# Loading and ordering of the first two layers: packed input transfers, a split mixing step, and a changed order on four engines

## The chip, the core and the metric

The kernel runs on one core of a Trainium2 chip. The metric is the device time of one execution in microseconds (us); the lower the better. The core has five engines with instruction streams of their own, which meet only at semaphores: TensorE (PE, matmuls, with its weight loads, PEld, shown apart), VectorE (DVE), ScalarE (ACT), GpSimd (POOL) and SyncE (SP), which here only issues DMA transfers. All data starts in HBM and ends there.

## The reference

Eight sequences of 128 tokens with 128 features go through four residual layers. `cond_8` (8 x 8) steers all of them:

```python
# layer 0: a base product plus a mixture of eight rank-16 adapters
out = einsum('btc,oc->bto', x, W_base) + b_base
lora = einsum('bter,eor,be->bto', einsum('btc,erc->bter', x, As), Bs, w)
x = x + out + lora * 2
# layer 1: eight weight matrices, masked, mixed per sequence
w_bot = einsum('bg,got->bot', y, weight * mask)
x = x + einsum('bnt,bot->bno', x, w_bot) + bias
# layer 2: gated MLP (128 -> 512 -> 128), top 2 of 8 experts per sequence, plus a shared one
x = x + sum_top2(w_e * mlp_e(x)) + mlp_shared(x)
# layer 3: gated MLP (128 -> 256 -> 128) of the single best expert, with biases
x = x + mlp3_best(x)
```

## The kernel before

Everything is held transposed: features on the 128 partitions, the 1024 tokens (8 sequences of 128) along the row, in two halves of 512. Each engine's program is written out by hand, in order, and each `wait_ge` names a semaphore; nothing is reordered by a scheduler.

**Layer 0.** The adapters and the base product are folded into one 128 x 128 matrix per sequence. VectorE (L363, sequences 0 to 3, in two instructions) and ScalarE (L272, sequences 4 to 7) scale the adapters' second factor into `b_mix`; TensorE's `mix0` (L575, three matmuls) multiplies by the first factor; VectorE's `weights0` (L374, once for each half) adds the base matrix plus identity, `base_i`, which GpSimd makes (L247). `product0` (L595, four matmuls for each half) applies the matrices to the tokens `x_t`, and ScalarE's `stream1` (L283) adds the bias.

**Layer 1.** `mix1_part` (L587) multiplies eight 128 x 128 blocks of the weights, four to a half, by a small spread-out matrix `mix1` of the conditions; VectorE's `weights1` (L382, once for each half) multiplies by the mask. `product1` (L603) needs both halves of these weights and its half of `x1_t`; VectorE's `stream2` (L424) makes the new tokens twice, rounded to the matmul's faster type (`x2_h`) and in full (`x2_t`); `stream2_rest` (L429) makes the difference `x2_l`.

**The shared expert of layer 2** runs first among the experts. Its three weight blocks (gate, up, down; n = 0, 1, 2) are split in the same way: ScalarE's `round_shared(n)` (L278) makes the high part, GpSimd's `shared_low_part(n)` (L250) the low part. TensorE's first matmul pair (L635 and L636, `shared_high(0, 0)`) needs `x2_h` and both parts of block 0; the next pair, `shared_high(0, 1)`, needs both parts of block 1 (`sh_high` and `sh_low` at 2). Then the products with `x2_l` follow (L644), and the down products (L651 to L654).

**Routing** runs on VectorE: `route_first` and `leave_first` (L392 to L397), then `route_second` (L401 to L404, whose last instruction signals `val2_ready`) and `rank_second` (L408). GpSimd waits for `val2_ready`, does `shared_low_part(0)`, then turns the ranks into expert numbers (L256, `routed`), then does blocks 1 and 2. SyncE waits for `routed` before it loads the experts' weights (L193, L201). ScalarE's exponential (L286) needs `route_second` too.

**The rest**, from about 27 us on, is one pass over the sequences with the routed experts (L664, L674) and layer 3 (L687, L701), with weights loaded two sequences ahead. The change does not touch it.

**Loads.** SyncE's queue issues, in order: `head` (the adapters and the conditions; its first 64 partitions, the others come from ScalarE's queue), `rest` (conditions for the routing, base matrix, mask, biases), the first half of layer 1's weights with `mix1` (L180), the first half of the tokens (L181), the second half of the weights (L182), the second half of the tokens (L183), and the shared expert's down block (L184). ScalarE's queue issues its half of `head`, and after its `b_mix` work the gate block and the up block (L274). Ahead of all its work TensorE runs six warm-up matmuls on a tile of zeros (L570) that VectorE sets (L357).

Of the kernel before, what the change touches and what calls it, by code (L numbers as in the profile page):

```python
# [5 lines left out]
B, S, C = 8, 128, 128  # L6
E = 8
R = 16
# [21 lines left out]
W1A = MIX // 2 + B * OH  # L30


def build(nc, x, head, rest_in, w1, shared, skill, layer3, out):
# [8 lines left out]
    with ctx:  # L42
# [33 lines left out]
        a_sb, b_sb, wcol = head_sb[:, 0:C], head_sb[:, C:2 * C], head_sb[:, 2 * C:HEAD]  # L76
        rest_sb = sb("rest_sb", [128, REST])
        condb, base_t, mask_t, b0col, b1col, bias3 = (rest_sb[:, at:at + n] for at, n in REST_PARTS)
# [3 lines left out]
        w1_sb = sb("w1_sb", [128, MIX + B * OH])  # L82
        mix1 = w1_sb[:, MIX // 2:W1A]
# [40 lines left out]
        x_loaded = [sem("x_loaded0"), sem("x_loaded1")]  # L124
        w1_in = [sem("w1_in0"), sem("w1_in1")]
        shared_in = [sem(f"shared_in{n}") for n in range(3)]
# [11 lines left out]
        warm_ready = sem("warm_ready")  # L138
# [98 lines left out]
        def _(pool):  # L237
# [20 lines left out]
            shared_low_part(1)  # L258
            shared_low_part(2)
# [7 lines left out]
        def _(act):  # L267
            act.dma_start(head_sb[64:128, :], head[64:128, :]).then_inc(head_in, 16)
            act.preload_act_table(ACT.Exp)
            act.wait_ge(head_in, 32)  # L270
            for b in range(HALF, B):
                act.activation(b_mix[:, b, :], b_sb, ACT.Copy, scale=wcol[:, b:b + 1]).then_inc(b_mixed2, 1)  # L272
            for n in range(2):
                act.dma_start(shared_sb[:, n, :], shared[:, n, :]).then_inc(shared_in[n], 16)  # L274

            def round_shared(n):
                act.wait_ge(shared_in[n], 16)
                act.activation(shared_h[:, n, :], shared_sb[:, n, :], ACT.Copy).then_inc(sh_high, 1)  # L278
# [63 lines left out]
        def _(dve):  # L342
# [14 lines left out]
            dve.memset(warm[:, :], 0.0).then_inc(warm_ready, 1)  # L357
            cond3 = condb.rearrange("p (b e) -> p b e", e=E)

            dve.wait_ge(head_in, 32)  # L360
# [5 lines left out]
            dve.wait_ge(rest_landed, 16)  # L366
# [11 lines left out]
            def weights1(h):  # L378

                dve.wait_ge(p1_done, h + 1)  # L380
# [186 lines left out]
        def _(pe):  # L567
            pe.wait_ge(warm_ready, 1)
            for _ in range(WARM):
                pe.matmul(bank[6][:, 0:128], warm[:, :], warm[:, :], start=True, stop=True)  # L570
# [9 lines left out]
            def mix1_part(h):  # L580

                pe.wait_ge(w1_in[0], 16)
                if h == 1:
                    pe.wait_ge(w1_in[1], 16)
                for n in range(OL // 2):
                    at = h * W1A + C * n
                    mm = pe.matmul(bank[5 + h][:, 128 * n:128 * (n + 1)], w1_sb[:, at:at + C], mix1, start=True, stop=True)  # L587
                mm.then_inc(p1_done, 1)
# [215 lines left out]
```

## Time and profile before

| | |
|---|---|
| time, median of 3 runs (lowest, highest) | 88.49 us (88.18, 88.63) |
| the profiled execution's own time | 87.75 us |
| its span, first to last instruction | 85.9 us |
| TensorE busy | 82.2 us (96%) of 618 matmul passes |
| VectorE, ScalarE, GpSimd busy | 47.7, 30.8, 15.5 us |
| read from HBM, written to it | 17.95 MB, 0.52 MB |

The profiled execution lies 0.74 us below the median of the runs. A matmul on fp32 data appears as two passes in the trace, so the six warm-up matmuls are twelve entries; one on the rounded type is one entry. A line of the time view stands for a row of like instructions: its second number is the time from the first one's start to the last one's end, and "xN" their count. Matmul entries overlap each other, so the start of a weight load is the better mark of TensorE's place in its program.

### The profile page before, as it was taken

The numbers are of one execution on the slowest core, as the hardware profiler recorded it, in microseconds if no ns is written. First come the engines' busy times: TensorE is split into PE (matmuls) and PEld (weight loads), VectorE is DVE, ScalarE is ACT, GpSimd is POOL, SyncE is SP. The second block draws the span as 40 slices with busy tenths as digits, with TensorE's granted clock in tenths as the row PEclk, the third lists the DMA queues.
The fourth block names the chain that finished last, engine by engine and source line by source line (L and its number), as shares of the span: only waits on it lengthen the run. The fifth ranks groups of instructions, "written<-read, shape, count | busy, mean of one in ns | idle before, by whom it ended". The sixth has DMA issues, their size and how long they took to land.

```text
span 85.9 us, 1921 instructions
## 1 busy us (share of the span) xinstructions
PE 82.2 (96%) x618; PEld 77.5 (90%) x618; DVE 47.7 (55%) x110; ACT 30.8 (36%) x55; POOL 15.5 (18%) x20
## 2 busy tenths in 40 slices
PE   5999899999999999999999999999999999999980
PEld 5978898888888999999999999999999999999970
DVE  0489439853533999329338447456465564563270
ACT  3702783777555520221221222212402402408320
POOL 3010773098666900000000000000000000000000
PEclk9999999999999999999999999999999999999999
DMA  0899318799920000596679899879998988717102
GB/s 7 214 358 312 143 23 326 266 325 425 402 72 0 0 0 4 132 331 272 206 269 328 253 296 306 302 264 312 337 346 316 299 279 315 289 41 163 50 0 61
DMA packets 5927, 18.57 MB, mean 216 GB/s; under 512 B 672, under 2 KB 1952, under 8 KB 5920
## 3 DMA queue, kind: packets, MB, share of 16 engines
q1 hardware_dynamic: 5552, 17.88, 61.0%
q10 hardware_dynamic: 368, 0.59, 2.1%
q8 instruction: 4, 0.07, 0.3%
q14 instruction: 3, 0.02, 0.2%
HBM read 17.95 MB, written 0.52 MB: 215 GB/s over the span
## 4 chain that ended last, share of the span: by engine, by line
PE 87%; DMA 6%; SPq 3%; issue 1%; DVE 0%
PE bank L664 33%; PE bank L674 17%; PE bank L687 9%; DMA w_sb<-in_w 6%; PE bank L701 4%; PE bank L635 4%; PE bank L636 4%; PE bank L644 4%; PE bank L603 2%; PE bank L652 2%; PE bank L654 2%; PE bank L651 2%; PE bank L587 1%; PE bank L595 1%; SPq L179 1%; SPq L178 1%
## 5 line engine op out<-in xcount | busy, mean ns | idle before, releaser
L664 PE MATMUL bank<-x_t,pair_w 128*128 128x128 f32 (+1 forms) x256 | 31.2, 275 | 0.0
L664 PEld LDWEIGHTS bank<-x_t,pair_w 128*128 128x128 f32 x256 | 30.0, 192 | 0.2
L300 ACT ACTIVATE gelu<-bank 128x512 f32<-128x512 f32 x24 | 14.2, 596 | 32.5 <-PE bank L664 27.8
L468 DVE SCALAR_TENSOR_TENSOR hid<-gelu,wsel,bank 128x512 f32<-128x512 f32 x16 | 12.0, 748 | 18.5 <-PE bank L664 18.4
L674 PE MATMUL bank<-hid,pair_w 128*128 128x128 f32 x128 | 16.9, 275 | 0.0
L674 PEld LDWEIGHTS bank<-hid,pair_w 128*128 128x128 f32 x128 | 15.7, 192 | 0.1
L263 POOL TENSOR_TENSOR hid_l<-hid,hid_h 128x512 fp32r<-128x512 f32 x8 | 10.2, 1289 | 6.3 <-ACT hid_h L323 6.3
L466 DVE TENSOR_TENSOR hid<-gelu,bank 128x512 f32<-128x512 f32 x8 | 5.5, 688 | 6.3 <-ACT gelu L300 3.8
L687 PE MATMUL bank<-x_t,w 128*128 128x128 f32 x64 | 8.7, 276 | 0.0
L687 PEld LDWEIGHTS bank<-x_t,w 128*128 128x128 f32 x64 | 7.9, 192 | 0.2 <-issue 0.2
L635 PE MATMUL bank<-x_h,shared_h 128*128 128x512 f32 x16 | 6.3, 396 | 0.0
L636 PE MATMUL bank<-x_h,shared_l 128*128 128x512 f32 x16 | 6.2, 390 | 0.0
L304 ACT ACTIVATE tanh<-half 128x256 f32<-128x256 f32 x6 | 2.5, 416 | 10.1 <-DVE half L497 10.1
L323 ACT ACTIVATE hid_h<-hid 128x512 fp32r<-128x512 f32 x8 | 5.0, 627 | 1.0 <-DVE hid L466 0.9
L701 PE MATMUL bank<-hid,w 128*128 128x128 f32 x32 | 4.9, 279 | 0.0
L644 PE MATMUL bank<-x_l,shared_h 128*128 128x512 f32 x16 | 4.8, 389 | 0.0
L250 POOL TENSOR_TENSOR shared_l<-shared_sb,shared_h 128x512 fp32r<-128x512 f32 x3 | 3.8, 1279 | 4.9 <-ACT shared_h L278 4.8
L701 PEld LDWEIGHTS bank<-hid,w 128*128 128x128 f32 x32 | 4.2, 191 | 0.1
L504 DVE SCALAR_TENSOR_TENSOR gate<-bank,bsel,half 128x128 f32<-128x128 f32 x12 | 3.7, 347 | 0.6
L570 PE MATMUL bank<-warm 128*128 128x128 f32 x12 | 2.9, 434 | 1.0 <-DVE warm L357 1.0
L497 DVE TENSOR_SCALAR half<-bank,bsel 128x128 f32<-128x128 f32 x12 | 3.6, 343 | 0.0
L570 PEld LDWEIGHTS bank<-warm 128*128 128x128 f32 x12 | 2.6, 329 | 1.0 <-DVE warm L357 1.0
(67 smaller groups left out, 76.6 us busy)
## 6 DMA issues: line engine op xcount, KB each, us to landing
pair_w<-in_skill SPq DMA_DIRECT2D x16, 768.0 KB, 5.8
w<-in_layer SPq DMA_DIRECT2D x8, 384.0 KB, 6.0
x_t<-in_x SPq DMA_DIRECT2D x2, 256.0 KB, 5.0
shared_sb<-in_shared ACTq DMA_DIRECT2D x2, 256.0 KB, 5.5
out_x<-out_sb SPq DMA_DIRECT2D x8, 64.0 KB, 4.6
w_sb<-in_w SPq DMA_DIRECT2D x1, 320.0 KB, 3.7
w_sb<-in_w SPq DMA_DIRECT2D x1, 256.0 KB, 5.6
shared_sb<-in_shared SPq DMA_DIRECT2D x1, 256.0 KB, 6.4
```

What stands on the lines that cost most here:

```text
L263: pool.tensor_tensor(hid_l[:, k % 3, :], hid[:, k % 2, :], hid_h[:, k % 3, :].bitcast(fp32), ALU.subtract).then_inc(hid_low, 1)
L300: act.activation(gelu[:, n, :], ps[:, :], ACT.Gelu_apprx_tanh).then_inc(gelu_ready, 1)
L466: dve.tensor_tensor(hid[:, n, :], gelu[:, n, :], shu_ps(k)[:, :], ALU.mult).then_inc(hid_ready, 1)
L468: dve.scalar_tensor_tensor(hid[:, n, :], gelu[:, n, :], wsel[:, bass.DynSlice(weight, 1)], u_ps[n][:, :], ALU.mult, ALU.mult).then_inc(hid ...
L570: pe.matmul(bank[6][:, 0:128], warm[:, :], warm[:, :], start=True, stop=True)
L635: pe.matmul(ps[:, :], shared_h[:, m, 128 * t:128 * (t + 1)], high, start=True, stop=False)
L636: pe.matmul(ps[:, :], shared_l[:, m, 128 * t:128 * (t + 1)], high, start=False, stop=False)
L644: pe.matmul(ps[:, :], shared_h[:, m, 128 * t:128 * (t + 1)], x2_l[:, N * h:N * (h + 1)], start=False, stop=True).then_inc(done, 1)
L664: mm = pe.matmul(ps[:, S * t:S * (t + 1)], pair_w[:, slot, n, 128 * t:128 * (t + 1)], x2_t[:, columns(b)], start=True, stop=True)
L674: mm = pe.matmul(acc_ps[:, 0:S], pair_w[:, slot, 2, C * t:C * (t + 1)], hid[:, k, S * t:S * (t + 1)], start=(k == 0 and t == 0), stop=(k = ...
L687: pe.matmul(ps[:, S * c:S * (c + 1)], w3[:, q, n, 128 * c:128 * (c + 1)], x3_t[:, q, :], start=True, stop=True).then_inc(done, 1)
L701: mm = pe.matmul(out_ps[:, 0:S], w3[:, q, 2, C * c:C * (c + 1)], hid3[:, q, c, :], start=(c == 0), stop=(c == HC - 1))
```

## The change

- **Loads.** `head` is one transfer over 128 partitions, issued by SyncE, and now holds the conditions for the routing too. ScalarE's queue starts with a new array `first`: `mix1` and the first two of layer 1's eight weight blocks. `rest` loses the routing's conditions and gains the other six blocks. The tokens are one transfer, third on SyncE's queue. After its `b_mix` work ScalarE's queue issues gate and up as one transfer, then down. So there are six transfers where there were ten; the bytes are the same, 2.2 MB.
- **Warm-up.** The zeros are a broadcast of a constant that exists before the program starts; VectorE's instruction and the wait for it go.
- **TensorE.** Two mixing blocks come ahead of `mix0`, the other six behind it, and `product0(0)` and `product0(1)` follow without a mixing part between them. Both wait for all tokens.
- **VectorE.** `route_second` and `rank_second` move behind `weights0(1)`, `weights1(0)` and `weights1(1)`.
- **ScalarE.** `round_shared(0)` comes first, then `stream1(0)`, the exponential, `stream1(1)`, and only then `round_shared(1)`.
- **GpSimd.** `shared_low_part(2)` also waits for the first half of `x2_l`.

```diff
-HEAD = 2 * C + B
-_WIDTHS = [B * E, C, C, 1, 1, (2 * HC + 1) * E]
+HEAD = 2 * C + B + B * E
+_WIDTHS = [C, C, 1, 1, (2 * HC + 1) * E]
-MIX = OL * C
+EARLY = 2
+FIRST = B * OH + EARLY * C
...
-        warm = sb("warm", [128, 128])
+        zeros = nc.const_aps.tensor(0.0, [128, 128], fp32)
...
-            sp.dma_start(head_sb[0:64, :], head[0:64, :]).then_inc(head_in, 16)
+            sp.dma_start(head_sb[:, :], head[:, :]).then_inc(head_in, 16)
             sp.dma_start(rest_sb[:, :], rest_in[:, :]).then_inc(rest_landed, 16)
-            sp.dma_start(w1_sb[:, 0:W1A], w1[:, 0:W1A]).then_inc(w1_in[0], 16)
-            sp.dma_start(x_t[:, 0:N], x[:, 0:N]).then_inc(x_loaded[0], 16)
-            sp.dma_start(w1_sb[:, W1A:MIX + B * OH], w1[:, W1A:MIX + B * OH]).then_inc(w1_in[1], 16)
-            sp.dma_start(x_t[:, N:2 * N], x[:, N:2 * N]).then_inc(x_loaded[1], 16)
-            sp.dma_start(shared_sb[:, 2, :], shared[:, 2, :]).then_inc(shared_in[2], 16)
+            sp.dma_start(x_t[:, :], x[:, :]).then_inc(x_loaded, 16)
...
             shared_low_part(1)
+            pool.wait_ge(x2_low, 1)
             shared_low_part(2)
...
-            act.dma_start(head_sb[64:128, :], head[64:128, :]).then_inc(head_in, 16)
+            act.dma_start(first_sb[:, :], first[:, :]).then_inc(first_in, 16)
...
-            for n in range(2):
-                act.dma_start(shared_sb[:, n, :], shared[:, n, :]).then_inc(shared_in[n], 16)
+            act.dma_start(shared_sb[:, 0:2, :], shared[:, 0:2, :]).then_inc(gate_up_in, 16)
+            act.dma_start(shared_sb[:, 2, :], shared[:, 2, :]).then_inc(shared_down_in, 16)
...
-            act.wait_ge(shifted_ready, 2)
-            act.activation(expo_all[:, :], shifted_all[:, :], ACT.Exp).then_inc(expo_ready, 1)
             round_shared(0)
             act.wait_ge(rest_landed, 16)
             stream1(0)
+            act.wait_ge(shifted_ready, 2)
+            act.activation(expo_all[:, :], shifted_all[:, :], ACT.Exp).then_inc(expo_ready, 1)
+            stream1(1)
             round_shared(1)
-            stream1(1)
             round_shared(2)
...
             weights0(0)
-            route_second()
-            rank_second()
             weights0(1)
             weights1(0)
             weights1(1)
+            route_second()
+            rank_second()
...
-            pe.wait_ge(head_in, 32)
+            pe.wait_ge(first_in, 16)
+            mix1_part(0, EARLY)
+            pe.wait_ge(head_in, 16)
             mix0(0, HALF // 2, b_mixed, 1)
             mix0(HALF // 2, HALF, b_mixed, 2)
             mix0(HALF, B, b_mixed2, HALF)
-            mix1_part(0)
+            pe.wait_ge(rest_landed, 16)
+            mix1_part(EARLY, OL)
             product0(0)
-            mix1_part(1)
             product0(1)
```

TensorE's rows from the first mixing work to the first product of layer 1. Before (L575 is `mix0`, L587 the mixing of layer 1, L595 `product0`):

```order
L575 MATMUL bank<-b_mix,head_sb 128x256 [waits b_mixed,head_in]
L575 MATMUL bank<-b_mix,head_sb 128x256 [waits b_mixed]
L575 MATMUL bank<-b_mix,head_sb 128x512 [waits b_mixed2]
L587 MATMUL bank<-w_sb 128x128 [waits w1_in0]
L587 MATMUL bank<-w_sb 128x128 x3
L595 MATMUL bank<-x_t,p 128x128 [waits x_loaded0,p0_ready]
L595 MATMUL bank<-x_t,p 128x128 x3
L587 MATMUL bank<-w_sb 128x128 [waits w1_in1,w1_in0]
L587 MATMUL bank<-w_sb 128x128 x3
L595 MATMUL bank<-x_t,p 128x128 [waits x_loaded1,p0_ready]
```

And of the changed kernel (L570 is `mix0`, L581 the mixing of layer 1, L590 `product0`):

```order
L581 MATMUL bank<-first_sb 128x128 [waits first_in]
L581 MATMUL bank<-first_sb 128x128
L570 MATMUL bank<-b_mix,head_sb 128x256 [waits b_mixed,head_in]
L570 MATMUL bank<-b_mix,head_sb 128x256 [waits b_mixed]
L570 MATMUL bank<-b_mix,head_sb 128x512 [waits b_mixed2]
L581 MATMUL bank<-first_sb,rest_sb 128x128 [waits rest_landed]
L581 MATMUL bank<-first_sb,rest_sb 128x128 x5
L590 MATMUL bank<-x_t,p 128x128 [waits x_loaded,p0_ready]
L590 MATMUL bank<-x_t,p 128x128 x3
L590 MATMUL bank<-x_t,p 128x128 [waits x_loaded,p0_ready]
```

Two blocks moved ahead of `mix0`, the four of the second half moved ahead of `product0(0)`, and one wait for all tokens stands where two waits for half of them stood.

ScalarE's rows between its `b_mix` work and the table load, before (L286 is the exponential, L278 `round_shared`, L283 `stream1`):

```order
L286 ACTIVATE expo_all<-shifted_all 128x72 [waits shifted_ready]
L278 ACTIVATE shared_h<-shared_sb 128x512 [waits shared_in0]
L283 ACTIVATE x_t<-bank,rest_sb 128x512 [waits x1_done,rest_landed]
L278 ACTIVATE shared_h<-shared_sb 128x512 [waits shared_in1]
L283 ACTIVATE x_t<-bank,rest_sb 128x512 [waits x1_done]
L278 ACTIVATE shared_h<-shared_sb 128x512 [waits shared_in2]
```

And of the changed kernel (L274 is `round_shared`, L279 `stream1`, L285 the exponential):

```order
L274 ACTIVATE shared_h<-shared_sb 128x512 [waits gate_up_in]
L279 ACTIVATE x_t<-bank,rest_sb 128x512 [waits x1_done,rest_landed]
L285 ACTIVATE expo_all<-shifted_all 128x72 [waits shifted_ready]
L279 ACTIVATE x_t<-bank,rest_sb 128x512 [waits x1_done]
L274 ACTIVATE shared_h<-shared_sb 128x512 [waits gate_up_in]
L274 ACTIVATE shared_h<-shared_sb 128x512 [waits shared_down_in]
```

The second `round_shared` now stands behind the second `stream1`, and the exponential between the two `stream1`.

## Rows read from the trace of the kernel before

**Rows 1.** Chain that ended last, in order: start us, us, what.
```profile
3.17 5.58 DMA w_sb<-in_w
8.74 0.14 issue
8.88 1.13 PE bank L587 x8
```

**Rows 2.** Stretches: us, busy time and count by engine, PEclk, DMA share, GB/s.
```profile
2.00:4.00 2.00, 2.00 (x11) 1.94 (x10) 0.76 (x2) 1.40 (x4) 0.00 (x0) 1.00 0.80 194
4.00:6.50 2.50, 2.50 (x6) 1.75 (x7) 2.10 (x7) 0.47 (x2) 0.46 (x1) 1.00 0.93 349
6.50:8.00 1.50, 1.50 (x13) 1.32 (x12) 1.40 (x7) 0.26 (x1) 0.00 (x0) 1.00 0.86 276
8.00:10.00 2.00, 1.74 (x15) 1.46 (x13) 0.77 (x2) 1.60 (x3) 0.96 (x1) 1.00 0.71 274
12.90:25.00 12.10, 12.10 (x56) 10.01 (x56) 7.29 (x11) 7.53 (x14) 7.22 (x6) 1.00 0.86 322
```

**Rows 3.** Groups to 14 us, by form: xcount | busy us, mean ns.
```profile
L570 PE MATMUL bank<-warm 128*128 128x128 f32 x12 | 2.9, 434 | 1.0 <-DVE warm L357 1.0
...
L595 PE MATMUL bank<-x_t,p 128*128 128x128 f32 x16 | 2.2, 280 | 0.0
```

**Rows 4.** TensorE's weight loads in time: start us, us, engine, line.
```profile
3.73 2.20 PEld L575 LDWEIGHTS bank<-b_mix,head_sb 128*128 128x128 f32 x6
...
6.25 0.19 PEld L587 LDWEIGHTS bank<-w_sb 128*128 128x128 f32 x1 [0.31 <-DMA w_sb<-in_w]
...
7.46 0.97 PEld L595 LDWEIGHTS bank<-x_t,p 128*128 128x128 f32 x8
...
8.85 0.97 PEld L587 LDWEIGHTS bank<-w_sb 128*128 128x128 f32 x8 [0.42 <-issue]
...
9.94 0.97 PEld L595 LDWEIGHTS bank<-x_t,p 128*128 128x128 f32 x8
...
10.83 2.08 PEld L603 LDWEIGHTS bank<-x_t,p 128*128 128x128 f32 x16
...
13.18 0.19 PEld L635 LDWEIGHTS bank<-x_h,shared_h 128*128 128x128 f32 x1
```

**Rows 5.** The other engines in the same stretch, in time.
```profile
4.22 0.46 POOL L247 TENSOR_TENSOR base_i<-rest_sb,ident 128x128 f32<-128x128 f32 x1 [2.67 <-DMA rest_sb<-in_rest]
...
6.51 0.21 DVE L401 TENSOR_REDUCE m<-rest 128x8 f32<-128x64 f32 x1
...
7.35 0.22 DVE L408 TENSOR_REDUCE rank<-val 128x8 f32<-128x64 f32 x1
...
9.04 1.28 POOL L250 TENSOR_TENSOR shared_l<-shared_sb,shared_h 128x512 fp32r<-128x512 f32 x1 [4.36 <-ACT shared_h L278]
...
10.05 0.69 DVE L382 TENSOR_TENSOR p<-bank,rest_sb 128x512 f32<-128x512 f32 x1 [1.28 <-PE bank L587]
...
10.69 1.27 POOL L250 TENSOR_TENSOR shared_l<-shared_sb,shared_h 128x512 fp32r<-128x512 f32 x1
...
11.14 0.69 ACT L283 ACTIVATE x_t<-bank,rest_sb 128x512 f32<-128x512 f32 x1 [0.90 <-PE bank L595]
11.72 0.62 ACT L278 ACTIVATE shared_h<-shared_sb 128x512 fp32r<-128x512 f32 x1
...
12.42 1.29 POOL L250 TENSOR_TENSOR shared_l<-shared_sb,shared_h 128x512 fp32r<-128x512 f32 x1 [0.46 <-ACT shared_h L278]
```

**Rows 6.** Transfers: queue, KB each, us from issue to landing (median).
```profile
x_t<-in_x SPq DMA_DIRECT2D x2, 256.0 KB, 5.0
shared_sb<-in_shared ACTq DMA_DIRECT2D x2, 256.0 KB, 5.5
...
head_sb<-in_head ACTq DMA_DIRECT2D x1, 66.0 KB, 2.4
```

**Rows 7.** SyncE's first load of an expert, in time.
```profile
11.58 1.48 SPq L193 DMA_DIRECT2D pair_w<-in_skill  x2
```

More of the change, by code:

```diff
@@ L21, with build @@
 LOWEST = -3.0e38
-HEAD = 2 * C + B
-_WIDTHS = [B * E, C, C, 1, 1, (2 * HC + 1) * E]
+HEAD = 2 * C + B + B * E
+_WIDTHS = [C, C, 1, 1, (2 * HC + 1) * E]
 REST_PARTS = [(sum(_WIDTHS[:n]), width) for n, width in enumerate(_WIDTHS)]
 REST = sum(_WIDTHS)
-MIX = OL * C
+EARLY = 2
+FIRST = B * OH + EARLY * C
 WARM = 6
-W1A = MIX // 2 + B * OH
-def build(nc, x, head, rest_in, w1, shared, skill, layer3, out):
+def build(nc, x, first, head, rest_in, shared, skill, layer3, out):
     fp32, fp32r, i32 = mybir.dt.float32, mybir.dt.float32r, mybir.dt.int32
@@ L75, in build @@
         head_sb = sb("head_sb", [128, HEAD])
-        a_sb, b_sb, wcol = head_sb[:, 0:C], head_sb[:, C:2 * C], head_sb[:, 2 * C:HEAD]
-        rest_sb = sb("rest_sb", [128, REST])
-        condb, base_t, mask_t, b0col, b1col, bias3 = (rest_sb[:, at:at + n] for at, n in REST_PARTS)
+        a_sb, b_sb, wcol = head_sb[:, 0:C], head_sb[:, C:2 * C], head_sb[:, 2 * C:2 * C + B]
+        condb = head_sb[:, 2 * C + B:HEAD]
+        first_sb = sb("first_sb", [128, FIRST])
+        mix1 = first_sb[:, 0:B * OH]
+        rest_sb = sb("rest_sb", [128, REST + (OL - EARLY) * C])
+        base_t, mask_t, b0col, b1col, bias3 = (rest_sb[:, at:at + n] for at, n in REST_PARTS)
         bias_t = bias3.rearrange("p (n e) -> p n e", e=E)
         base_i = sb("base_i", [128, C])
-        warm = sb("warm", [128, 128])
-        w1_sb = sb("w1_sb", [128, MIX + B * OH])
-        mix1 = w1_sb[:, MIX // 2:W1A]
+        zeros = nc.const_aps.tensor(0.0, [128, 128], fp32)
         p1 = sb("p1", [C, B, C])
@@ L123, in build @@
         head_in, rest_landed = sem("head_in"), sem("rest_landed")
-        x_loaded = [sem("x_loaded0"), sem("x_loaded1")]
-        w1_in = [sem("w1_in0"), sem("w1_in1")]
-        shared_in = [sem(f"shared_in{n}") for n in range(3)]
+        first_in, x_loaded = sem("first_in"), sem("x_loaded")
+        gate_up_in, shared_down_in = sem("gate_up_in"), sem("shared_down_in")
         sh_high, sh_low = sem("sh_high"), sem("sh_low")
@@ L355, in over_b @@
                 return a.unsqueeze(1).broadcast_to([128, B, a.shape[1]])
-            dve.memset(warm[:, :], 0.0).then_inc(warm_ready, 1)
             cond3 = condb.rearrange("p (b e) -> p b e", e=E)
-            dve.wait_ge(head_in, 32)
+            dve.wait_ge(head_in, 16)
             for first in range(0, HALF, HALF // 2):
@@ L378, in weights1 @@
             def weights1(h):
+                dve.wait_ge(rest_landed, 16)
                 dve.wait_ge(p1_done, h + 1)
@@ L567, in _ @@
         def _(pe):
-            pe.wait_ge(warm_ready, 1)
             for _ in range(WARM):
-                pe.matmul(bank[6][:, 0:128], warm[:, :], warm[:, :], start=True, stop=True)
+                pe.matmul(bank[6][:, 0:128], zeros, zeros, start=True, stop=True)
             def mix0(first, last, mixed, count):
@@ L578, in mix0, with mix1_part @@
                     mm.then_inc(p0_done, 1)
[L580 to L588, printed above, removed]
+            def mix1_part(begin, end):
+                for a in range(begin, end):
+                    h, n = a // (OL // 2), a % (OL // 2)
+                    weights = (first_sb[:, B * OH + C * a:B * OH + C * (a + 1)] if a < EARLY else
+                               rest_sb[:, REST + C * (a - EARLY):REST + C * (a - EARLY + 1)])
+                    mm = pe.matmul(bank[5 + h][:, 128 * n:128 * (n + 1)], weights, mix1, start=True, stop=True)
+                    if n == OL // 2 - 1:
+                        mm.then_inc(p1_done, 1)
             def product0(h):
                 pe.wait_ge(p0_ready, h + 1)
-                pe.wait_ge(x_loaded[h], 16)
+                pe.wait_ge(x_loaded, 16)
                 for n in range(HALF):
```

16 lines of the change are left out of this document (7 added, 9 removed).

## The prediction

> **What bounds the kernel now.** I read the chain of waits first, then the busy time in stretches, then the order in time of each engine up to 14 us. From 12.9 to 25 us TensorE is busy for all of 12.1 us [rows 2], and the chain holds nothing but TensorE from there to the last matmul. So whatever moves the start of the shared expert's stream moves the end by the same amount, and nothing behind it gives it back. The kernel has a front, up to the weight load of `shared_high(0, 1)` at 13.18 us [rows 4], and a tail that is carried along. The change edits only the front. I use that one weight load as the finish line, because its operands are the ones that the change makes later.
>
> In the front the chain is a transfer, the second half of layer 1's weights, issued at 3.17 us and there 5.58 us later, and then TensorE [rows 1]. From the weight load of `mix1_part(1)` at 8.85 the marks are 9.94, 10.83 and 13.18 [rows 4]. Ahead of it TensorE was nearly full as well: `mix0` from 3.73, the first mixing part at 6.25, `product0(0)` at 7.46, whose eight passes end near 8.4. That is the first thing to see: before 8.85 TensorE waits only some 0.4 us, the gap in front of that row. A better load order can win 0.4 us and little more.
>
> The second thing is the clock. The granted clock reads 1.00 in every stretch [rows 2], but the durations say otherwise: a 128-column fp32 pass takes 434 ns in the warm-up and 280 ns in `product0` [rows 3], and twelve warm-up passes fill 2.9 us, 244 ns each, where eight passes of `product0` load their weights in 0.97 us [rows 4], 112 ns from one to the next. So I take TensorE to be at 1.2 GHz, the lower of its two levels, through the warm-up and most of `mix0`, and at 2.4 GHz from about 6 us, where a weight load has come down to 0.19 us. A pass placed ahead of 6 us costs twice what it costs behind it.
>
> **The change part by part.**
>
> *First landings.* `head` was two transfers of 66 KB (68,000 bytes each), the later one there 2.4 us after its issue at 0.7, so at 3.1 [rows 6]. Now `head` is 168,000 bytes and `first`, 197,000, moves beside it, all on the same engines. The extra 230,000 bytes need 0.6 to 1.2 us at 349 to 194 GB/s [rows 2], of which `head` bears about half. I take 3.8 for both (3.4 to 4.3).
>
> *TensorE up to the products.* The warm-up no longer waits for VectorE and starts 0.2 us earlier, which only lengthens the wait for the first data. At 3.8 the two mixing blocks run: four passes at 244 ns [rows 3], 1.0 us. `mix0` thus starts at about 4.8, 1.0 us later than in rows 4; `b_mix` is ready by then. Of the 1.0 us of slow work pushed past the clock's rise half is given back, so `mix0` ends about 0.5 us later, at 7.1, where 6.6 was its end before. Then six blocks, twelve passes at 112 ns, 1.35 us: TensorE reaches `product0(0)` at 8.5. Moving the two blocks forward used an idle slot that was not there; what it bought is 0.45 us of fast work behind, and what it cost is 1.0 us of slow work in front, half of it recovered, so about nothing.
>
> *The tokens.* They are third on SyncE's queue and both products wait for all of them. Ahead of or with them go `head`, `first` and `rest` (546,000 bytes) and the tokens themselves (524,000): 1,435,000 bytes, and up to 524,000 of gate and up, which ScalarE's queue adds from about 5.2. The kernel before had moved 388,000 by 4.0, 1,260,000 by 6.5, 1,674,000 by 8.0 and 2,222,000 by 10 (each the GB/s by the length of the stretch [rows 2]). On that curve 1,435,000 are reached at 7.1 and 1,959,000 at 9.0; with 0.5 us until the semaphore, the tokens land between 7.6 and 9.5. The stretch up to 4.0 should be better than 194 GB/s, since two large transfers are queued from the start: at 349 GB/s it is 1.0 us of head start. Against this stands that a transfer is there only when the slowest engine has finished. I take 8.4, the upper middle, and keep 7.2 and 9.4.
>
> *A rule of the Trainium skill.* The rows show 194 GB/s while the small transfers ran and 349 GB/s just after [rows 2], which speaks for fewer and longer ones. The Trainium skill ("DMA: Bandwidth & Descriptors", Rules for kernel authors) says the same, that many small transfers should be coalesced and that two over disjoint halves of the partitions are pointless; by its fixed cost of about 2 us and 436 GB/s, an estimate for 1.43 MB is 5.3 us from the first issue, so tokens at 6.0. The same page of the Trainium skill also says (Issuing engines are not separate DMA queues) that the queues of all engines interleave on the same 16 DMA engines, and that is what speaks against the change: gate and up take their share while the tokens are under way. No row shows the tokens alone.
>
> *Start of the products.* TensorE is ready at 8.5, the tokens are there at 8.4: call it S = 8.5. `product0(1)` follows 0.9 us later without a pause, at P = 9.4, where it was 9.94. From there the old spacing to the finish line is 3.24 us (9.94 to 13.18 [rows 4]), which gives 12.64: a gain of 0.54.
>
> *Rounding of the up block.* The finish line also needs both parts of block 1. ScalarE now does `stream1(1)` first. It came 1.2 us after the weight load of `product0(1)` (9.94 to 11.14), the next rounding 0.58 us later, GpSimd's part 0.70 us after that, and took 1.28 us [rows 5]. From P that is 9.4 + 1.2 + 0.58 + 0.70 + 1.28 = 13.16. Before, the part was done at 11.96, 1.2 us ahead of its use; that cover is gone.
>
> *GpSimd's own queue.* It may be later still. `route_second` now stands behind `weights1(1)`. That instruction came 1.2 us after the first weight load of its four blocks (8.85 to 10.05) and took 0.69 [rows 5]; its blocks now load from 7.6, so it runs from 8.8 to 9.5. `route_second` takes 0.84 (6.51 to 7.35): `val2_ready` at 10.34. There GpSimd starts block 0, and block 1 follows 1.65 us later (9.04 to 10.69), with the ranks between: 11.99, done at 13.27, and TensorE sees it at about 13.32. The same order delays the ScalarE exponential (needs `shifted_ready` at about 9.8, while `stream1(1)` could start at 10.6: hidden) and `routed`, from 10.6 to about 11.85. SyncE's first load of an expert moves from 11.58 [rows 7] to about 12.9; its consumer sits behind 25 us and its load took under 6, so this is free.
>
> *The rest.* `base_i` waits for a larger `rest`, there at 4.1 before [rows 5], about 5.4 now; `weights0(0)` needs it at 6.3. GpSimd's block 2 waits for `x2_l`, near 14 us, and has until the first down product, behind 18 us. Gate and up land near 9.0; `round_shared(0)` takes 0.6 and `stream1(0)` is wanted at 9.7. All at nothing, each with cover of 0.1 to 4 us; the thinnest is gate and up, which cost from 9.2 on.
>
> **The sum.** 13.32 against 13.18: 0.54 won on TensorE, 0.68 lost in the wait for the up block's low part, +0.14 us. On the profiled execution that is a span of 86.04 and a time of 87.9; the median of the runs lies 0.74 above the profiled one, so I forecast 88.49 + 0.15 = 88.65.
>
> **The rivals.**
>
> *Tokens late (slower).* If the tokens land after 8.5, every microsecond counts in full, and TensorE starts from a standstill, 1.09 instead of 0.9 to the next row [rows 4]. At 9.3 the products start at 9.35, P is 10.44 and the finish line 10.44 + 3.76 + 0.05 = 14.25: +1.1, 89.6. For it: the transfer that ended the front before took 5.6 us [rows 1], the half-token transfers 5.0 [rows 6], and now more bytes stand ahead. Against: the slack 194 GB/s at the beginning. It decides from 8.5.
>
> *Both early (faster).* With tokens at 7.5 and a clock that rises right behind the warm-up, `mix0` ends at about 6.1 (ScalarE's last `b_mix` is what it waits for), six blocks end at 7.5, S = 7.6, P = 8.6, and the finish line is 12.4: -0.75, 87.75. For it are the stretches at 349 GB/s; it needs the early rise too, and the rows put that at 6. The coalescing rule of the Trainium skill ("DMA: Bandwidth & Descriptors", Rules for kernel authors) points this way, but for the tokens alone.
>
> *Low part in time (faster).* If `shared_high(0, 1)` does not wait, the gain of 0.54 stays: 87.95. For it is only that GpSimd's spans are rough; against it is that the rounding stands behind `stream1(1)` in the program.
>
> *Clock late (slower).* Slow work now lies in front. If the rise comes at 7.5, `mix0` is done at 7.9 and the products start at 9.25, +0.85: 89.35. The rows show one rise only. The Trainium skill ("TensorE: Matmul & The Clock Gate", Part 1) states that the throttled clock is the default and that activity releases it; by that rule the earlier warm-up does no harm, and no run here shows when the rise comes in another execution.
>
> **How the numbers follow.** My forecast, 88.3 to 88.9: 0.46. Tokens late: 0.22. Clock late: 0.08. Both early: 0.15. Low part in time: 0.09. The range that holds 8 in 10 runs from 87.9 to 89.4; left out are most of "both early" and the upper half of the two slow cases. A measurement of this kernel can tell about 0.5%, 0.44 us, from no change. So faster 0.24, same 0.46, slower 0.30.
>
> **What would show it.** In the changed kernel's trace: the tokens' landing and the weight load of the first `product0` at about 8.5; `product0(1)` 0.9 behind it; an idle TensorE of 0.5 to 0.7 us between the first and the second pair of L632 and L633, released by GpSimd's `shared_l`; that `shared_l` started by ScalarE's rounding or by GpSimd's own queue at about 12; no TensorE gap behind it. I am wrong if TensorE stands idle ahead of `product0`, if the 128-column passes of the mixing are slow beyond 7 us, or if the second pair follows the first at once.

## The result and the profile after

| | before | changed |
|---|---|---|
| median over all executions beside each other | 88.28 us (14) | 87.61 us (14) |
| ratio of the changed kernel to the one before | | 0.991, 95% interval 0.989 to 0.994 |
| profiled execution: time, span | 87.75, 85.9 us | 87.69, 85.9 us |

The change makes the kernel faster by 0.9%, 0.7 to 0.8 us, and the time lies below the forecast range. The ratio leaves out executions more than 1.5% above the fastest of their kernel: three of the changed kernel's fourteen, at 88.53, 89.60 and 292.65 us, the last of unknown cause. A second series of twelve executions, beside 22 others of the kernel before (median 88.36), gave a median of 87.87 and a ratio of 0.995 (0.990 to 0.999), half the gain of the first series; the two intervals overlap.

The two profiled executions have the same span, although the medians are 0.67 us apart. That is the puzzle of this case, and the trace of the changed kernel alone doesn't solve it. First the busy time in stretches of the changed kernel (columns as in rows 2):

```profile
2.00:4.00 2.00, 1.67 (x9) 1.37 (x8) 0.20 (x1) 0.64 (x2) 0.00 (x0) 1.00 0.86 315
4.00:6.50 2.50, 2.50 (x10) 2.11 (x11) 2.06 (x9) 1.08 (x4) 0.46 (x1) 1.00 1.03 420
6.50:8.00 1.50, 1.50 (x12) 1.26 (x11) 1.39 (x3) 0.18 (x1) 0.00 (x0) 1.00 0.88 347
8.00:10.00 2.00, 2.00 (x20) 2.00 (x19) 1.78 (x7) 1.03 (x2) 0.00 (x0) 1.00 0.00 0
```

Where rows 2 have 194, 349, 276 and 274 GB/s, it is now 315, 420, 347 and nothing: the same 2.2 MB are over two microseconds earlier. The tokens land 4.8 us after their issue at 1.65, at 6.5 us.

The chain that ended last, changed kernel (start us, us, what; the finish line of the prediction is the wait that ends at 13.1):

```profile
0.72 3.23 DMA first_sb<-in_first
...
3.99 1.23 PE bank L581 x4
5.22 1.87 PE bank L570 x6
7.09 1.35 PE bank L581 x12
...
8.53 0.69 DVE p L377
...
9.72 0.24 DVE val L399
...
10.03 1.27 POOL shared_l L245
...
11.38 0.21 POOL chosen L251
...
11.67 1.30 POOL shared_l L245
...
13.10 0.47 PE bank L632
```

The landing of `first` at 3.95 us is the last one on it. Then it is TensorE's mixing work, VectorE's `weights1` and routing, and two of GpSimd's low parts: the chain that the prediction worked out, step for step. The weight loads of TensorE in time, where L581 is the mixing of layer 1, L570 `mix0`, L590 and L598 the products:

```profile
3.99 0.93 PEld L581 LDWEIGHTS bank<-first_sb 128*128 128x128 f32 x4 [0.63 <-DMA first_sb<-in_first]
...
4.80 1.46 PEld L570 LDWEIGHTS bank<-b_mix,head_sb 128*128 128x128 f32 x6
...
6.50 0.19 PEld L581 LDWEIGHTS bank<-first_sb,rest_sb 128*128 128x128 f32 x1 [0.24 <-issue]
...
8.15 1.87 PEld L590 LDWEIGHTS bank<-x_t,p 128*128 128x128 f32 x16
...
10.22 1.86 PEld L598 LDWEIGHTS bank<-x_t,p 128*128 128x128 f32 x16 [0.20 <-issue]
...
12.22 0.19 PEld L632 LDWEIGHTS bank<-x_h,shared_h 128*128 128x128 f32 x1
...
13.07 0.19 PEld L632 LDWEIGHTS bank<-x_h,shared_h 128*128 128x128 f32 x1 [0.55 <-issue]
```

The finish line is at 13.07 where rows 4 have it at 13.18. From 12.22 to 13.07 are 0.85 us where the kernel before needs 0.34: that is the forecast wait for block 1's low part.

### The profile page after: what moved, and what is told of

It is laid out like the page before. It is cut to its first block, busy times and chain, and to the rows that moved or that the text cites. A ratio compares the mean times of both kernels' runs of the same rounds, so it can differ in the third digit from the quotient of the medians.

```text
span 85.9 us, 1918 instructions
## 1 busy us (share of the span) xinstructions
PE 82.2 (96%) x618; PEld 77.3 (90%) x618; DVE 47.3 (55%) x109; ACT 30.7 (36%) x55; POOL 15.6 (18%) x20
## 4 chain that ended last, share of the span: by engine, by line
PE 87%; DMA 4%; POOL 3%; DVE 2%; issue 1%; DVEq 0%
PE bank L661 33%; PE bank L671 17%; PE bank L684 9%; PE bank L698 4%; PE bank L632 4%; PE bank L641 4%; PE bank L633 4%; DMA first_sb<-in_first 4%; PE bank L581 3%; POOL shared_l L245 3%; PE bank L570 2%; PE bank L649 2%; PE bank L648 2%; PE bank L651 2%; DVE p L377 1%
## 5 line engine op out<-in xcount | busy, mean ns | idle before, releaser
L632 PEld LDWEIGHTS bank<-x_h,shared_h 128*128 128x128 f32 x16 | 3.0, 188 | 1.2 <-issue 0.6
L564 PE MATMUL bank<-const-float32-0.0 128*128 128x128 f32 x12 | 2.9, 432 | 0.8 <-PEq L793 0.8
```

Source lines behind the costliest of these rows:

```text
L632: pe.matmul(ps[:, :], shared_h[:, m, 128 * t:128 * (t + 1)], high, start=True, stop=False)
```

## The experiments

All ratios are to runs of the kernel before on the same chip. I read the same few marks in every trace. The finish line is the weight load of `shared_high(0, 1)`; "mix0" is the time from the first to the last of its six weight loads, which is short where the clock rises early in it.

| kernel | mix0, us | first product0 | finish line | span | span less finish line |
|---|---|---|---|---|---|
| before, first trace | 2.20 | 7.46 | 13.18 | 85.9 | 72.7 |
| before_3rd | 1.40 | 8.47 | 13.72 | 86.5 | 72.8 |
| before_4th | 1.37 | 7.94 | 13.85 | 86.6 | 72.8 |
| changed, first trace | 1.46 | 8.15 | 13.07 | 85.9 | 72.8 |
| after_again | 2.25 | 9.96 | 14.88 | 87.5 | 72.6 |
| loads_only3 | 2.21 | 9.49 | 15.06 | 87.9 | 72.8 |
| loads_only_warm8 | 1.87 | 7.92 | 13.18 | 85.9 | 72.7 |
| mix0_first | 2.20 | 10.11 | 15.01 | 88.9 | 73.9 |
| mix0_first_warm8 | 1.52 | 8.23 | 13.14 | 85.8 | 72.7 |
| loads_early | 1.33 | 7.20 | 12.45 | 85.2 | 72.8 |
| loads_early_warm7 | 1.77 | 7.83 | 13.09 | 85.9 | 72.8 |
| both_early3 | 1.64 | 8.47 | 13.25 | 86.0 | 72.8 |
| split_loads | 2.25 | 10.04 | 14.96 | 87.6 | 72.6 |
| orders_only3 | 1.95 | 9.87 | 14.72 | 87.5 | 72.8 |

The last column is the first finding: in thirteen of fourteen traces the tail takes 72.6 to 72.8 us. (In mix0_first, whose profiled execution took 90.69 us, TensorE waits once more, 0.95 us at 56.3, for an expert's weights.) All differences lie in the front.

### The kernel before, twice more

> The kernel before once more, for a second profiled execution. Theory 1 (the profiled execution of before was an unusually good one: 87.75 us where 14 runs have a median of 88.28 and a lowest of 88.02): span 86.2 to 86.8, and the weight load of shared_high(0, 1) at 13.5 to 14.0 us instead of 13.18, because the second half of layer 1's weights lands later. Theory 2 (the front is the same in every execution, and the 0.7 us that the change won against the median came from elsewhere): finish line at 13.1 to 13.3 and the extra time behind it.

> A third profiled execution of the kernel before. Theory: its time follows the landing of the second half of layer 1's weights (8.7 us with span 85.9, 9.0 with span 86.5) and of the first half of the tokens (6.6 and 8.4); the rise of the clock, 6.0 and 4.2 us, doesn't show in it. A span of 86.2 to 86.8 with these landings at 8.8 to 9.3 and 6.6 to 8.6 supports it.

No edit. The times are 88.30 and 88.42 us, in the middle of the executions of before (median 88.4 and 88.36), where the first profiled one, at 87.75, was below the lowest of fourteen. In both the clock rises earlier than in the trace that I predicted from, and the finish line is later all the same, by 0.54 and 0.67 us. Weight loads of before_3rd, then of before_4th:

```profile
3.71 1.40 PEld L575 LDWEIGHTS bank<-b_mix,head_sb 128*128 128x128 f32 x6
...
8.47 0.97 PEld L595 LDWEIGHTS bank<-x_t,p 128*128 128x128 f32 x8 [1.65 <-DVE p L374]
...
10.49 0.97 PEld L595 LDWEIGHTS bank<-x_t,p 128*128 128x128 f32 x8 [0.16 <-issue]
...
13.72 0.19 PEld L635 LDWEIGHTS bank<-x_h,shared_h 128*128 128x128 f32 x1
```

```profile
6.42 0.97 PEld L587 LDWEIGHTS bank<-w_sb 128*128 128x128 f32 x8 [1.24 <-DMA w_sb<-in_w]
...
7.94 0.97 PEld L595 LDWEIGHTS bank<-x_t,p 128*128 128x128 f32 x8 [0.55 <-issue]
9.28 0.97 PEld L587 LDWEIGHTS bank<-w_sb 128*128 128x128 f32 x8 [0.37 <-issue]
```

The chain of before_3rd, and the transfers of layer 1's weights in before_4th (KB, us to landing):

```profile
2.69 5.68 DMA x_t<-in_x
...
8.51 1.13 PE bank L595 x8
9.63 0.89 PE bank L587 x8
```

```profile
w_sb<-in_w SPq DMA_DIRECT2D x1, 320.0 KB, 4.2
w_sb<-in_w SPq DMA_DIRECT2D x1, 256.0 KB, 6.0
```

TensorE idles 1.65 us ahead of `product0(0)` in the one (the first tokens land at 8.37; the label names VectorE's `weights0(0)`, which was done by 6.7), and 1.24, 0.55 and 0.37 us in the other. The late half of the weights needs 6.0 us where the first trace had 5.58 [rows 1]. So in both of these executions, which lie in the middle of the times, the kernel before waits for landings, and a clock that rises earlier only makes TensorE wait longer. The ranges of both expectations held. The reason given in the first one was only half right: in before_3rd it is the first half of the tokens that ends the wait, and the late half of the weights, there at 9.04, delays nothing. The long executions of the kernel before, 11 of 33 at 88.8 us or more in the two series beside mix0_first and after_again, were not traced, and what makes them long is not shown.

### The loads alone

> The changed kernel's six transfers with the orders of before on TensorE (mix0 first, a mixing part between the two products), VectorE, ScalarE and GpSimd; the constant-zero warm-up stays. If the gain of the change comes from the loads alone (tokens at 6.4 us in the changed kernel's trace, nothing is late), TensorE runs from mix0 at 4.2 us to the first layer without a pause and does not wait for the low part of block 1: finish line at 12.4 to 12.7, 87.0 to 87.2 us, 0.4 to 0.6 below the changed kernel. If the new orders carry the gain: at or above the changed kernel, 87.6 to 88.3.

```diff
-            pe.wait_ge(first_in, 16)
-            mix1_part(0, EARLY)
             pe.wait_ge(head_in, 16)
             mix0(0, HALF // 2, b_mixed, 1)
...
+            pe.wait_ge(first_in, 16)
...
-            mix1_part(EARLY, OL)
+            mix1_part(0, OL // 2)
             product0(0)
+            mix1_part(OL // 2, OL)
             product0(1)
```

This is against the changed kernel; on VectorE, ScalarE and GpSimd the lines that the change moved stand in their old places. Measured: 89.13 us in the median of 11, ten of them at 88.83 and above, one at 86.96. Neither reading had this. The finish line is at 15.06, and the cause is seen in TensorE's loads and in the chain:

```profile
4.42 2.21 PEld L569 LDWEIGHTS bank<-b_mix,head_sb 128*128 128x128 f32 x6 [1.05 <-DMA head_sb<-in_head]
```

```profile
4.45 3.75 PE bank L569 x6
8.20 1.71 PE bank L580 x8
9.90 1.07 PE bank L589 x8
```

Without the early blocks TensorE stands idle for 1.05 us between the warm-up and `mix0`, which needs `b_mix` and so begins 0.57 us behind the landing of `head` at 3.85. Then everything up to about 10 us runs at the pace of the 1.2 GHz level: `mix0` takes 3.75 us on the chain (1.87 in the changed kernel), eight passes of the mixing 1.71 (0.89 for eight in the row of loads_only_warm8 below). The granted clock reads 1.00 all the while.

> The changed kernel with the two early mixing blocks moved back behind mix0: TensorE waits for b_mix from the end of the warm-up at 3.6 us to about 4.4. Theory A (the gap keeps TensorE's clock at its lower level, as in the kernel with the loads alone, where mix0 began at 4.42 and passes stayed slow to about 10 us): first product0 at 9 us or later, finish line (weight load of shared_high(0, 1)) at 14.5 to 15.5, 89 us and more in most executions. Theory B (what cost that kernel its time was another of the old orders, not the gap): the blocks' place is worth nothing, 87.4 to 88.0 us, as the changed kernel.

> The same with eight warm-up matmuls instead of six, so that the warm-up ends at 4.6 us and touches mix0. Theory A (what counts is that TensorE doesn't pause): the clock rises by 4.5 to 6.5 us again and the time is that of the changed kernel, 87.2 to 87.9. Theory B (it is the blocks themselves, mixing done early, that count): as slow as without them and with six, 89.

> The kernel with the loads alone (six transfers, all orders of before, mix0 first), which took 89.13 us with a clock that rose at 10.1 us, with eight warm-up matmuls in place of six. Theory A (its loss was the pause of 1 us in TensorE ahead of mix0, and with it the late clock): rise at 4.5 to 6.5, finish line 12.4 to 12.7, 87.0 to 87.5 us, so that the loads alone, with the pause filled, carry the whole gain. Theory B (the old orders don't suit the new loads): above 88.

```diff
 # mix0_first, from the changed kernel
-            pe.wait_ge(first_in, 16)
-            mix1_part(0, EARLY)
...
+            pe.wait_ge(first_in, 16)
...
-            mix1_part(EARLY, OL)
+            mix1_part(0, OL)
 # mix0_first_warm8 is mix0_first, loads_only_warm8 is loads_only3, each with
-WARM = 6
+WARM = 8
```

mix0_first: median 89.13 us of 6, four at 88.9 and above, two at 87.3 and 87.5. mix0_first_warm8: 87.73 of 6, none above 88.29, ratio 0.994 (0.988 to 1.000). loads_only_warm8: 87.52 of 12, none above 88.33, ratio 0.990 (0.986 to 0.994). The loads of `mix0` in mix0_first and in loads_only_warm8:

```profile
4.31 2.20 PEld L570 LDWEIGHTS bank<-b_mix,head_sb 128*128 128x128 f32 x6 [0.94 <-DMA head_sb<-in_head]
```

```profile
4.61 1.87 PEld L569 LDWEIGHTS bank<-b_mix,head_sb 128*128 128x128 f32 x6 [0.39 <-issue]
```

And the chain of loads_only_warm8:

```profile
0.76 3.75 PE bank L563 x16
...
4.64 2.67 PE bank L569 x6
7.30 0.89 PE bank L580 x8
8.19 0.89 PE bank L589 x8
```

Two more matmuls on zeros, 0.85 us of useless work in a gap, bring back 1.4 and 1.6 us in the median (the second pair ran on two chips, beside executions of before with medians of 88.40 and 88.36). Theory A held each time, with misses in its numbers: of mix0_first three of six, and not most, were at 89 us or more, and loads_only_warm8 came at 87.52, at the edge of 87.0 to 87.5. It wasn't the early blocks as mixing work that mattered, but that TensorE had something to do between the warm-up and `mix0`; and with the gap filled the new loads, with the zeros that need no VectorE, carry the whole gain of the change without its new orders. How much the constant zeros bring alone was not measured. The finish line of loads_only_warm8 came at 13.18, later than the 12.4 to 12.7 that I expected, with a `mix0` of 1.87 us that was not the quickest.

### The changed kernel again, and where its time spreads

> The changed kernel once more, beside the next two on one chip. Theory: TensorE's front is no longer set by a landing but by its own work and the clock, so that the finish line (weight load of shared_high(0, 1)) is where the rise of the clock puts it: 13.0 to 13.1 with a rise at 5.4 us, as in the first trace, later by half of what the rise is later. Time 87.3 to 87.8 us, with single executions at 89 when the rise comes late.

No edit. Twelve executions: nine from 87.11 to 88.31, and three at 89.32, 89.62 and 90.32, the first of them profiled. TensorE's loads in that one:

```profile
4.17 0.93 PEld L581 LDWEIGHTS bank<-first_sb 128*128 128x128 f32 x4 [0.81 <-DMA first_sb<-in_first]
...
4.98 2.25 PEld L570 LDWEIGHTS bank<-b_mix,head_sb 128*128 128x128 f32 x6
...
9.96 1.87 PEld L590 LDWEIGHTS bank<-x_t,p 128*128 128x128 f32 x16
...
14.88 0.19 PEld L632 LDWEIGHTS bank<-x_h,shared_h 128*128 128x128 f32 x1 [0.54 <-issue]
```

`mix0` is slow to its end and beyond, the first product starts at 9.96 instead of 8.15, though the tokens were there at 6.7. The expectation held: nothing of this front waits for a landing after 4.2 us, and the time follows the clock. The changed kernel leaves a pause of 0.6 to 0.9 us behind its warm-up, and of the five traces with early blocks and six warm-up matmuls three show the early rise and two (this one and split_loads) the late one. All ten traces with the new loads, in the order of TensorE's idle time behind the warm-up; the rise is the start of the first weight load of some 190 ns, where a slow one takes 333:

| kernel | idle behind the warm-up, us | rise, us |
|---|---|---|
| mix0_first_warm8 | 0.15 | 5.3 |
| loads_only_warm8 | 0.39 | 6.3 |
| loads_early_warm7 | 0.46 | 6.4 |
| changed, first trace | 0.63 | 5.4 |
| loads_early | 0.69 | 5.4 |
| both_early3 | 0.76 | 6.0 |
| after_again | 0.81 | 9.0 |
| split_loads | 0.88 | 9.0 |
| mix0_first | 0.94 | 9.1 |
| loads_only3 | 1.05 | 10.3 |

The late rises are those with the four longest pauses. In the changed kernel the pause ends with the landing of `first`, at 3.95 us in the first trace and 4.13 in this one, and between these two traces lie 1.8 us at the finish line. Whether the length of the pause itself decides, or something that goes along with it, was not varied any finer. With the longest pauses, 0.94 and 1.05 us in the traces, 14 of 17 executions took 88.8 us or more; with seven or eight warm-up matmuls, none of 24. How the clock rose in the executions without a trace is not shown.

> The changed kernel's loads and its two early blocks on TensorE, but the old orders otherwise: a mixing part between the two products, routing ahead of the second weights0 on VectorE, the exponential first and round_shared(1) ahead of stream1(1) on ScalarE. It differs from the kernel with the loads alone by the early blocks only. Theory A (gap and clock): it loses that kernel's 2 us, and without the wait for block 1's low part the finish line is at 12.5 to 12.8, 86.9 to 87.2 us, below the changed kernel. Theory B (the old orders cost it): 88.5 and more.

> The best version so far (new loads, two early blocks, old orders otherwise; 87.36 us) with a seventh warm-up matmul, which fills the 0.7 us between the end of the warm-up and the landing of the first blocks. If the pause there makes the rise late in some executions (one of six at 89.28): median 87.1 to 87.3 and none above 88. If it only pushes the blocks back: 87.4 to 87.6.

```diff
 # loads_early, from the changed kernel: routing, exponential and round_shared(1) in the old places, no GpSimd wait for x2_l, and
-            mix1_part(EARLY, OL)
-            product0(0)
+            mix1_part(EARLY, OL // 2)
+            product0(0)
+            mix1_part(OL // 2, OL)
             product0(1)
 # loads_early_warm7: also
-WARM = 6
+WARM = 7
```

loads_early: 87.36 us of 6, ratio 0.989 (0.983 to 0.994), with one at 89.28. loads_early_warm7: 87.20 of 6, none above 87.85, ratio 0.989 (0.983 to 0.995). The loads of loads_early:

```profile
4.87 1.33 PEld L569 LDWEIGHTS bank<-b_mix,head_sb 128*128 128x128 f32 x6
...
12.11 0.19 PEld L632 LDWEIGHTS bank<-x_h,shared_h 128*128 128x128 f32 x1
12.45 0.19 PEld L632 LDWEIGHTS bank<-x_h,shared_h 128*128 128x128 f32 x1
```

The second pair follows 0.34 us behind the first, where it is 0.85 in the changed kernel, and the finish line is 0.62 us ahead of the changed kernel's. Of these, 0.51 us are the wait for block 1's low part that is gone, and 0.11 are TensorE's earlier arrival at the first pair, 12.11 for 12.22. So the new orders on VectorE, ScalarE and GpSimd cost 0.51 us in the trace, where the prediction charged 0.68, and the loads pay for it. The finish line (12.45) and the median (87.36) both lie just outside what theory A gave; for loads_early_warm7 the first reading held. In the times the difference to the changed kernel is not resolved: the intervals overlap. loads_early_warm7 has the lowest median of all, 87.20 where after_again had 87.87 beside it, but the intervals of their ratios overlap too.

### The wait for the low part removed in another way

> The changed kernel with round_shared(1) directly behind round_shared(0) on ScalarE, and shared_low_part(0) and (1) on GpSimd ahead of the wait for the routing. If TensorE's pause between the first and the second shared pair (0.55 us in the changed kernel's trace) is all of it a wait for the low part of block 1, it goes, and nothing else is late: finish line at 12.5 instead of 13.07, ratio to the changed kernel 0.994, 87.0 us. If the pause only moves (VectorE's routing blocked beside GpSimd, or x2_h late): 87.4 to 87.7.

```diff
             round_shared(0)
+            round_shared(1)
             act.wait_ge(rest_landed, 16)
             stream1(0)
...
-            round_shared(1)
...
-            pool.wait_ge(val2_ready, 1)
             shared_low_part(0)
+            shared_low_part(1)
+            pool.wait_ge(val2_ready, 1)
...
-            shared_low_part(1)
```

87.70 us of 6, ratio 0.989 (0.984 to 0.995): no better than the changed kernel. ScalarE and the finish line in its trace:

```profile
9.07 1.15 ACT L274 ACTIVATE shared_h<-shared_sb 128x512 fp32r<-128x512 f32 x2 [3.88 <-DMA shared_sb<-in_shared]
...
10.13 0.67 ACT L279 ACTIVATE x_t<-bank,rest_sb 128x512 f32<-128x512 f32 x1
...
10.91 1.86 PEld L598 LDWEIGHTS bank<-x_t,p 128*128 128x128 f32 x16 [0.57 <-issue]
...
12.91 0.19 PEld L632 LDWEIGHTS bank<-x_h,shared_h 128*128 128x128 f32 x1
...
13.25 0.19 PEld L632 LDWEIGHTS bank<-x_h,shared_h 128*128 128x128 f32 x1
```

The wait between the pairs is gone; they follow each other at 0.34 us. But gate and up landed only at 9.05 in this execution (7.8 in the changed kernel's first trace), and both roundings now stand ahead of `stream1(0)`, so the first product of layer 1 waits 0.57 us where it waited 0.20. The second reading was right: the pause moved, to the wait for `stream1(0)`, and `x2_h` comes later for it. The 0.18 us by which this finish line lies behind the changed kernel's are 0.32 from a later start of the products (8.47 for 8.15, with a later rise of the clock) and 0.37 from this wait, less the 0.51 saved. With gate and up as early as 7.8 the wait might be shorter; no trace shows that.

### Rows and number of transfers; the orders alone

> The changed kernel with tokens in two transfers of 256 KB and gate, up and down in three: rows of 2 KB instead of 4 KB, the queues' order the same. If long rows make the loads quick (tokens complete at 6.5 and 7.8 us in two traces, 9.8 and 10.4 before): tokens complete at 8 us or later, 88 us or more. If it is the order (tokens third on a queue that is full from the start, the shared expert's blocks behind): tokens' second half by 7.9, 87.3 to 87.9 us, same as the changed kernel within 0.3%.

```diff
-            sp.dma_start(x_t[:, :], x[:, :]).then_inc(x_loaded, 16)
+            for h in range(2):
+                sp.dma_start(x_t[:, N * h:N * (h + 1)], x[:, N * h:N * (h + 1)]).then_inc(x_loaded[h], 16)
...
-            act.dma_start(shared_sb[:, 0:2, :], shared[:, 0:2, :]).then_inc(gate_up_in, 16)
-            act.dma_start(shared_sb[:, 2, :], shared[:, 2, :]).then_inc(shared_down_in, 16)
+            for n in range(3):
+                act.dma_start(shared_sb[:, n, :], shared[:, n, :]).then_inc(shared_in[n], 16)
```

Each product waits for its own half of the tokens. 87.45 us of 6, ratio 0.990 (0.984 to 0.996), as the changed kernel. The transfers of its trace (KB each, median us to landing):

```profile
shared_sb<-in_shared ACTq DMA_DIRECT2D x3, 256.0 KB, 4.4
x_t<-in_x SPq DMA_DIRECT2D x2, 256.0 KB, 4.6
```

The half-token transfers take 4.6 us where rows 6 have 5.0, and the second half is there at 6.8 us. Splitting the tokens and the shared blocks into rows of 2 KB costs nothing that these runs resolve. What it leaves in place are the one transfer for `head`, the new `first`, and the large `rest` with its rows of 4.3 KB. Which of these makes the first four microseconds quicker was not taken apart.

> The ten transfers of before with the changed orders on ScalarE, VectorE and GpSimd, and both mixing parts ahead of both products on TensorE (the two early blocks can't be had without their transfer, so they stay behind mix0). If loads carry the gain: the mixing waits for the late half of the weights with both products behind it, +0.8 us, and the low part of block 1 adds 0.6: about 89.5. If the orders carry it: below 88.3.

```diff
 # from the kernel before: the changed orders on ScalarE, VectorE and GpSimd, and on TensorE
             mix1_part(0)
-            product0(0)
             mix1_part(1)
+            product0(0)
             product0(1)
```

88.75 us of 12, ratio 1.002 (0.999 to 1.005). The direction of the first reading holds, since the orders win nothing without the loads, but the loss of 0.2% is not clear of zero, where I expected 1.1 us. In its trace the finish line is at 14.72, 0.9 to 1.0 later than in the two usual traces of before; that execution, at 89.29, was one of the longer ones. Why the median loses so little stays open.

## Why the prediction was wrong

**The sum was nearly right, its translation into a time was not.** From the first trace of before the prediction made a finish line of 13.32 and a profiled time of 87.9; measured are 13.07 and 87.69. The forecast of the median, 88.65, lies 1.04 us above the measured 87.61. About 0.2 us of this is the sum for the profiled execution. The step that failed is the last one of the sum: "the median of the runs lies 0.74 above the profiled one", added to the changed kernel as well, whose profiled execution lies 0.08 us above its median: 0.82 us. That distance (0.53 against the fourteen runs) was not an overhead common to both kernels. It was the landings of the kernel before, which in the trace that I had came early (5.58 us for the late weights, 3.9 for the first tokens) and in two other traces late (5.9 and 6.0 for the weights, 5.7 and 5.1 for the tokens). This is just what the change removes. Against the usual finish line of before, 13.72 and 13.85, the changed kernel's 13.07 is 0.65 to 0.78 us ahead, and the medians differ by 0.67. The two sides are few traces each, and the changed kernel's own finish line moves with the clock, so this match is good evidence and no exact account.

**What bounds the kernel.** "A better load order can win 0.4 us and little more" was read from one execution, in which TensorE waited 0.4 us. In before_4th it waits 1.24, 0.55 and 0.37 us in the same stretch, and loads_early, with the new loads and of the new orders only the two early blocks, has its finish line 1.3 to 1.4 us ahead of the two usual traces of before, and 0.73 ahead even of the first one. The claim that the tail is carried along unchanged held in thirteen of fourteen traces.

**First landings.** Forecast 3.8, measured 3.8 (`head`) and 3.95 (`first`). Right. What the prediction didn't ask is what a few tenths later do to the clock.

**TensorE up to the products.** Forecast 8.5, measured 8.15, with a clock that rose earlier within `mix0` (1.46 us for its loads where the first trace of before has 2.20). Right in mechanism, with some luck in the number: with the late rise the same point comes at 9.96. The two blocks took 0.8 us of weight loads and not 1.0. The prediction's 244 ns is 2.9 us by twelve, and the row's first entry is longer than the others; the warm-up's weight loads start some 213 ns apart (four more of them lengthen their row from 2.63 to 3.49 us). But "about nothing" for the early blocks missed what they are good for: without them the pause behind the warm-up grows from 0.63 to about 1 us and the kernel loses 1.5 us in the median. I had called them an idle slot that was not there; mix0_first shows the slot at 0.94 us.

**The tokens.** Forecast 8.4, measured 6.5 to 7.8. The term was too large by 0.6 to 1.9 us, because I laid the new transfers on the old curve, 349 GB/s at the best, where it ran at 420. Since TensorE came later anyway it changed nothing in the sum. The rival "tokens late", with 0.22, occurred in none of the ten traces with the new loads.

**Rounding, GpSimd's queue.** Forecast: the low part of block 1 starts at 11.99 and holds the second pair for 0.68 us. Measured: 11.67 and 0.51. Right in its mechanism, which is GpSimd's own queue behind `route_second`, and 0.17 us too large.

**Both early.** This rival, with 0.15, has the time nearest to the measured one, 87.75, and that is luck. Its tokens were early (6.5 where it asked for 7.5) and the clock rose earlier than in the first trace of before, but its finish line of 12.4 left out GpSimd's own queue, and 13.07 was measured. Its finish line, 0.7 us too early, and the 0.8 us added too much to get from a profiled time to the median cancel.

**Clock late.** It exists, as a matter of single executions (three of twelve in the second series) and not of the kernel's median: +1.8 us at the finish line in after_again, priced at 0.85, because the rise came near 9 us and not at 7.5. About the clock the Trainium skill ("TensorE: Matmul & The Clock Gate", Part 1) says that the throttled state is the default and that activity releases it; the pairs with six and with eight warm-up matmuls agree with it, 89.13 and 87.73 us. The same section says that the warm-up penalty is under 1% of a typical kernel; here the late rise costs 1.8 of 86 us at the finish line, 2%.

**The rule on coalescing.** The Trainium skill ("DMA: Bandwidth & Descriptors", Rules for kernel authors) would have many small transfers made one. The stretch from 2 to 4 us agrees, 315 GB/s where it was 194, though the packing changed size, rows and queues at once. That split_loads, with eight transfers instead of six, is as quick doesn't speak against the rule, since its transfers are still of 256 KB; it shows that coalescing the tokens and the shared blocks further brought nothing here.

## What to carry to other kernels

One profiled execution is one draw: before its distance to the median is added to a forecast, ask which waits of the chain vary between executions and whether the change removes them. When a front is bounded by a landing, TensorE's clock and its own queue are hidden behind it; once the landing is gone they set the time, and here a pause of a microsecond behind the warm-up cost more than the loads won. So fill such a pause with work, or with matmuls on zeros, up to the moment at which the first operands land.

## What the runs showed of the hardware

The granted clock in the records reads 1.00 in the first ten microseconds of every trace here, while the weight loads of 128-column fp32 passes start some 213 ns apart in the warm-up and 112 ns apart later, so the level has to be read from the durations of like instructions. With the old loads, where TensorE went on from the warm-up to `mix0` without a pause, the rise came at 6.3, 4.3, 4.3 and 5.6 us (before, before_3rd, before_4th, orders_only3). With the new loads it came between 5.3 and 6.4 us in six traces with a pause of 0.15 to 0.76 us, and between 9.0 and 10.3 us in four with a pause of 0.81 to 1.05 us. From 2 to 4 us the new packing moved 287 to 325 GB/s in ten traces, the old one 189 to 208 in four. Of the kernel before, the same transfer of tokens, 256 KB, was there 3.9, 5.7 and 5.1 us after its issue in three executions.
